# Attention stage of a fused layer on one core: q's first half projected in the third round, the turns of two score rows set later

## The reference

```
qkv = einsum('bse,ehd->bshd', xn, w_qkv)          # 16 heads of 64
q, k, v = split(qkv, 3, axis=-1)
logits = einsum('bqhd,bkhd->bhqk', q, k) / 8, masked to k <= q
probs = softmax(logits)
out = einsum('bshd,hde->bse', einsum('bhqk,bkhd->bqhd', probs, v), w_out)
```

## Time and profile before

| | |
|---|---|
| median of the runs | 3128.54 us |
| profiled execution | 3129.8 us |
| its span, first to last instruction | 3128.0 us |
| PE busy | 89% |
| DVE busy | 71% |
| POOL busy | 55% |
| ACT busy | 51% |
| mean granted TensorE clock over the span | 0.966 |

### The profile page before, as it was taken

One profiled execution on the slowest core, in us unless ns is written; L12 is line 12 of the kernel. 1 busy time (PEld: TensorE's weight loads), 2 busy tenths in 40 slices (PEclk: granted clock), 3 DMA queues, 4 the chain that ended last, 5 costly groups with the idle time before them and its releaser, 6 DMA issues. The chain is left out here.

```text
span 3128.0 us, 58978 instructions
## 1 busy us (share of the span) xinstructions
PE 2768.4 (89%) x20403; PEld 2239.2 (72%) x20403; DVE 2220.5 (71%) x4704; ACT 1589.8 (51%) x3674; POOL 1730.4 (55%) x2636
## 2 busy tenths in 40 slices
PE   4699999999988888888888888888888888888987
PEld 3589998999976666666666666666666666666665
DVE  8744344444347887788788788878887887888886
ACT  3454444444535555555555555555555555555553
POOL 3122221222117676677677666766776676677774
PEclk8799999999999999999999999999999999999999
DMA  7112221122126777677677767767776767677665
GB/s 243 43 54 71 79 71 58 61 76 73 58 61 158 164 170 175 163 165 172 169 170 169 181 156 165 172 171 163 168 184 152 168 166 186 146 168 189 162 168 137
DMA packets 253565, 440.11 MB, mean 141 GB/s; under 512 B 77649, under 2 KB 178001, under 8 KB 253281
## 3 DMA queue, kind: packets, MB, share of 16 engines
q1 hardware_dynamic: 216576, 327.82, 42.6%
q0 software_dynamic: 36704, 108.61, 13.6%
HBM read 102.80 MB, written 33.55 MB: 44 GB/s over the span
## 5 line engine op out<-in xcount | busy, mean ns | idle before, releaser
L1445 POOL TENSOR_SCALAR pr<-pr,rinv 128x512 f32<-128x512 f32 (+7 forms) x1024 | 751.5, 749 | 607.8 <-DVE rinv L1368 602.9
L1300 ACT ACTIVATE pr<-pr,negm 128x512 f32<-128x512 f32 (+7 forms) x1024 | 784.3, 769 | 496.0 <-DVE negm L1362 495.9
L1362 DVE CUSTOM_DVE_ANT_0 pr<-S,late 128x512 f32<-128x512 f32 (+7 forms) x1024 | 716.5, 751 | 108.0 <-PE S L1238 108.0
L1405 DVE STREAM_TRANSPOSE squares<-pr 128x512 f32<-128x512 f32 x764 | 639.4, 881 | 1.2 <-DMA pT<-squares 1.1
L1270 PE MATMUL O<-pT,vv 128*64 128x256 f32 (+1 forms) x5120 | 555.2, 369 | 25.6 <-ACT khf L1320 12.2
L1270 PEld LDWEIGHTS O<-pT,vv 128*64 128x64 f32 x5120 | 357.0, 140 | 218.8 <-issue 40.7
L832 DVE TENSOR_TENSOR hl<-h,hh 128x512 fp32r<-128x512 f32 x256 | 192.3, 752 | 315.5 <-ACT hh L793 306.7
L789 ACT ACTIVATE h<-pH,b1c 128x512 f32<-128x512 f32 x256 | 176.1, 688 | 365.6 <-PE pH L719 335.5
L731 PE MATMUL pY<-w2h,hh 128*128 128x256 f32 x1024 | 287.8, 281 | 2.5 <-DVE hl L832 2.5
L731 PE MATMUL pY<-w2l,hh 128*128 128x256 f32 x1024 | 289.0, 282 | 0.0
L731 PE MATMUL pY<-w2h,hl 128*128 128x256 f32 x1024 | 288.0, 281 | 0.0
(11 more groups left out here) (176 smaller groups left out, 6382.6 us busy)
## 6 DMA issues: line engine op xcount, KB each, us to landing
pT<-squares SPq DMA_DIRECT2D x768, 160.0 KB, 5.4
pT<-squares SPq DMA_DIRECT2D x756, 128.0 KB
pT<-squares POOLq DMA_DIRECT2D x256, 160.0 KB, 5.3
pT<-squares POOLq DMA_DIRECT2D x252, 128.0 KB
y<-yb SPq DMA_DIRECT2D x128, 128.0 KB, 1.7
wr<-in_L_attn_w_qkv SPq DMA_DIRECT2D x128, 128.0 KB, 2.4
x<-in_L_attn_x SPq DMA_DIRECT2D x16, 512.0 KB, 8.9
xn<-xn SPq DMA_DIRECT2D x16, 512.0 KB, 4.7
```

Of the source, the lines that this page charges most:

```text
L1300: e.activation(p, p, ACT.Exp, bias=negm[:, c0:c0 + 1], scale=-1.0, accum_out=rsum[:, c0:c0 + 1]).then_inc(expd.sem, 1)
L1362: e.tensor_tensor_reduce(room_of(n, i, h)[:, off:off + w], S[h][:, off:off + w], late[:, SEQ - w:], 1.0, -MASKED, ALU.add, ALU.min, negm[: ...
L1405: e.transpose(sq[g][:, :, 2 * h + i % 2, 0:KT, :], room_of(n, i, h)[:, OFFSET[i]:OFFSET[i] + KT * P].rearrange("p (k b i) -> p b k i", b=Q ...
L1445: e.tensor_scalar(p, p, rinv[:, c0:c0 + 1], 1.0, ALU.mult, ALU.mult).then_inc(scaled.sem, 1)
```

## The change

In step 8 PE now does p0 behind the scores of rows 5 and 0. t1 goes to step 11, behind o0 and o1 and ahead of the second run of O. In step 12 o2 follows the scores of row 6, and t0 follows in step 13. ACT and DVE read p0 in step 10, ahead of o0 on DVE; o1 is read in step 11, t1 in step 12 behind the copy of O, o2 in step 14. The banks of p1, p0, o2 and t0 change. The number of instructions is the same.

```
     STEP_OF = {"v0": 0, "xn": 1, "v1": 2,
                "p1": 4,
-               "t1": 8, "o0": 9, "o1": 10,
-               "t0": 12, "p0": 12, "o2": 13,
+               "p0": 8, "o0": 9, "o1": 10, "t1": 11,
+               "o2": 12, "t0": 13,
                "p2": 16, "p3": 17, "o3": 18}
-    ACT_STEP = {"v0": 2, "xn": 2, "v1": 4, "p1": 6, "t1": 8, "t0": 12, "p0": 13, "p2": 17, "p3": 18}
-    DVE_STEP = {"xn": 2, "p1": 6, "o0": 10, "o1": 10, "p0": 14, "o2": 15, "p2": 18, "p3": 19, "o3": STEPS}
-    BANK_OF = {"v0": 0, "xn": 2, "v1": 1,
-               "p1": 2,
-               "t1": 2, "o0": 1, "o1": 0,
-               "t0": 2, "p0": 1, "o2": 0,
-               "p2": 0, "p3": 1, "o3": 2}
+    ACT_STEP = {"v0": 2, "xn": 2, "v1": 4, "p1": 6, "p0": 10, "t1": 12, "t0": 13, "p2": 17, "p3": 18}
+    DVE_STEP = {"xn": 2, "p1": 6, "p0": 10, "o0": 10, "o1": 11, "o2": 14, "p2": 18, "p3": 19, "o3": STEPS}
+    BANK_OF = {"v0": 0, "xn": 2, "v1": 1, "p1": 0, "p0": 2, "o0": 1, "o1": 0, "t1": 2, "o2": 2, "t0": 1, "p2": 0, "p3": 1, "o3": 2}
```

## The result

| | before | after |
|---|---|---|
| median | 3129.86 us (4 runs, 3127.03 to 3131.67) | 3155.25 us (4 runs, 3150.42 to 3160.35) |
| ratio | | 1.0082, 95% interval 1.0063 to 1.0101 |
| span of the profiled execution | 3128.0 us | 3158.5 us |
| mean granted TensorE clock in it | 0.966 | 0.975 |

The change makes the kernel 0.8% slower, 25 us, though its clock is higher.

What follows compares the result with a forecast made beforehand. PE bounds the kernel, standing 2.59 us before t1, often with half clock behind. Units +22.7 us, edges about +1, batch units -5.6, clock 0: +18 us, median 3146, range 3112 to 3172.

Steps and rivals of the forecast that it cites:

- The wait that takes the other's place: Ahead of t1, PE's wait for POOL's scaling goes; a wait of 2.5 us for p0's readers on ACT and DVE replaces it.
- o0's wait: Behind p0, PE waits 0.56 us for DVE's ol before it can start o0.
- A clean unit: A unit without batch-start disturbance, at full clock, gets 0.42 us longer, to 33.8 us.
- The clock: Half clock behind the turn's stall keeps its share, 27 of 47 units at 1.46 us each, so nothing gained or lost.
- my own mark for being wrong: The prediction counts as wrong if, among other signs, the count of slow units moves by more than ten.
- Near the end: The 7 units whose wait was 1.29 us keep 2.4 GHz; each is 0.42 us longer.
- The batch's start: In the 7 units behind a batch's start the strips wait less: 0.8 us off each, between 0 and 3.
- The sum: All terms together: +18 us on the profiled 3129.8, a median of 3146 us.
- The rival on the other side: t1's wait goes with nothing in its place: unit 31.3 us, clock holds, 159 us less, 2987 us; chance 0.05.

Runs made afterwards that it cites:

- e1: Changed kernel with p0 read earlier, by ACT in step 8 and by DVE in step 9 (both were 10): 3039.06 us, ratio 0.9706.
- e2: Changed kernel with p0 read in step 8 by both ACT and DVE: 3010.7 us, ratio 0.9615.
- e5: Changed kernel with only ACT reading p0 in step 8, DVE still in step 10: 3063.24 us, ratio 0.9784.
- e3: Changed kernel with p0 in bank 1, o0 in bank 2, and DVE reading p0 in step 11: 3255.52 us, ratio 1.0389.
- e6: Changed kernel with t0 again ahead of o2 in PE's step 12: 3146.27 us, ratio 1.0042.
- e4: Kernel before with only t1 moved, to step 11 behind o0 and o1, read by ACT in step 12: 3115.44 us, ratio 0.9954.
- e8: Kernel before with only p0 moved, to step 8 ahead of t1, read there by ACT and DVE, banks p0 0, o2 1: 3038.84 us, ratio 0.9703.

## Why the prediction was right, point by point

- **The wait that takes the other's place: right.** I had t1 7.74 us behind the first score of rows 5 and 0 (1586.48 - 1578.74); it stands at 1663.08 - 1655.35 = 7.73. o0's wait is mostly 0.45 to 0.54 us for 0.56, and ACT's exponential starts 0.12 us behind its row minimum, as said. That p0's reading is the cause is shown by e1, e2 and e5, which move only this reading, and by e3, which moves it back and finds t1 behind it in a bank that is not p0's.
- **A clean unit: right in sign, too small.** Forecast +0.42, measured +0.78. PE needs 0.56 us from t1 to the run of O (I took the 0.38 of t1 to o0), 2.55 us from the scores of row 6 to the third run with t0 last (I had 2.43), and 1.65 instead of 1.57 from p1 to the first run. These three add up to 0.38, the missing 0.36 within rounding. The first two I had taken from the old order, in which other instructions stand next to each other. Of the second e6 gave 0.06 back; why the third grew is open.
- **The clock: the share was wrong.** I kept 27 slow units of 47; they are 12, each at 1.61 instead of 1.46 us, which is 20 us less loss. This met my own mark for being wrong, a count that moves by over ten. Near the end I expected none, and 5 of 7 came, behind a stall of 1.92 us where it had been 1.29 to 1.40: 8 us more. By the Trainium skill, page TensorE: Matmul & The Clock Gate, section Why this matters for your kernels, the gaps to avoid are those above about 3 us. The traces do not agree: half clock stands behind 2.35 us here as it did behind 2.58, and in e3 the clock stayed at full behind 14 of 47 gaps of 3.08 us.
- **The batch's start: right.** 0.68 us off each unit for 0.8. The wait ahead of the first run of O fell by 1.6 us, from 2.7 to 1.1 on the mean of the seven.
- **The sum.** Forecast +18 us, measured +25. Ordinary units: +37 by their clean length (forecast 20), -20 by the clock (forecast 0). Near the end: +14, of which 8 by the clock (forecast 3 and 0). Behind a batch's start: -5 (forecast -6). So the total came out near because a unit that was longer than I said was slowed by the clock less often than I said. The mechanism and the sign rest on runs, the size in part on luck.
- **The rival on the other side** (nothing takes the wait's place; 2987 us, at 0.05) is what e2 makes true in part by reading p0 in time: unit 31.80 us for 31.3, 3010.7 us. Its sum was also wrong by 18 us: the 2.1 us a unit are counted against the kernel before and have to come off 3128, not off the forecast of 3146, which gives about 2970.

## What to carry to other kernels

When a piece of work is pulled forward into a stall, pull forward the instructions that read its buffer too, on every engine: here the same change is 0.8% slower with q read in step 10 and 3.8% faster with q read in step 8. Look up who used the buffer last before each step that moves, and count in that engine's own queue what stands ahead of this reader; the profile's page may call such a wait "issue". Where one counter stands for many readings, a reading moved back delays everybody who waits for a later number.

## What the runs showed of the hardware that I had not expected

The clock: in the ordinary units half speed came behind 12 of 47 stalls of 2.35 us with a short one of 0.5 ahead, and behind 7 of 47 of the same kind in e6. It came behind 27 of 47 of 2.59 us (the kernel before), behind 27 of 47 of 2.12 us (e4) and behind 33 of 47 of 3.08 us (e3). So the length of the stall alone does not order these counts, and what does is open. Behind stalls of 1.1 us or less (e1, e2, e5, e8) no ordinary unit was slow. A slow stretch costs 1.61 us where it lies on a run of O (4.13 us for 2.60) and 1.46 where it lies on output projections. A switch from the turns' transposes straight to a run of O took PE 0.56 us, to an output projection 0.38.
